# Stacked two-part operands laid out anew in a cross-attention kernel, and one context remainder moved ahead of the maxima

## The reference

```python
# layer 0: one head, width 512, masked
q = x @ Wq.T + bq;  k = y @ Wk.T + bk;  v = y @ Wv.T + bv
scores = where(mask == 0, -1e9, q @ k.T)
x1 = softmax(scores) @ v + x
# layer 1: 16 heads of 32, on x1
Q, K, V = x1 @ Wq.T + bq, y @ Wk.T + bk, y @ Wv.T + bv      # split into heads
ctx = softmax(Q @ K.T / sqrt(32)) @ V                       # heads joined again
z = ctx @ W_o.T + b_o + x1
out = (z - mean(z)) / sqrt(var(z) + 1e-5) * gamma + beta
```

## Time and profile before

| | before |
|---|---|
| time, median of 3 runs | 422.56 us (421.71 to 424.55) |
| profiled execution: its time | 420.85 us |
| profiled execution: its span | 418.9 us |
| mean granted TensorE clock | 0.989 of full |
| TensorE matmuls busy (share of span) | 391.7 us (93%) |
| VectorE, ScalarE, GpSimd busy | 288.4, 264.0, 228.2 us |

### The profile page before, as it was taken

The page is one execution under the profiler, slowest core; times in us unless marked ns, Lnnn a source line. Parts: engine busy times, 40 slices in busy tenths (PEclk is TensorE's granted clock), DMA queues, the critical chain, the costliest instruction groups (busy, mean ns, idle before and its releaser), DMA issues.

```text
span 418.9 us, 12165 instructions
## 1 busy us (share of the span) xinstructions
PE 391.7 (93%) x4968; PEld 296.9 (71%) x4968; DVE 288.4 (69%) x703; ACT 264.0 (63%) x783; POOL 228.2 (54%) x249
## 2 busy tenths in 40 slices
PE   4999998799999999999999999999999999999990
PEld 4996765577777877777777777777778776677570
DVE  0145487468866996689867986698579866557656
ACT  0443777675678665867487657856786658565620
POOL 0400368225537753785568656774377547822766
PEclk9999999999999999999999999999999999899997
DMA  8993104400042301430042205130333012330112
GB/s 256 399 359 101 50 6 129 146 4 3 2 138 87 127 2 44 181 105 26 10 172 95 76 2 170 57 126 2 126 98 127 2 30 79 101 129 2 42 58 100
DMA packets 19229, 39.44 MB, mean 94 GB/s; under 512 B 1865, under 2 KB 5449, under 8 KB 18151
## 3 DMA queue, kind: packets, MB, share of 16 engines
q1 hardware_dynamic: 18599, 37.72, 26.1%
q10 hardware_dynamic: 576, 0.96, 0.8%
HBM read 26.49 MB, written 8.39 MB: 83 GB/s over the span
## 4 chain that ended last, share of the span: by engine, by line
PE 82%; DMA 6%; ACT 5%; POOL 2%; SPq 2%; DVE 2%; issue 1%; POOLq 0%
PE ps_q L910 21%; PE ps_out L975 20%; PE ps_t L935 13%; PE ps_s L924 7%; PE ps_pv L950 7%; PE ps_out L871 4%; DMA p_b<-p_l 4%; PE ps_s L847 4%; SPq L267 2%; ACT prob L494 1%; PE ps_pv L884 1%; DMA raw<-in_w0k 1%; ACT pt L503 1%; PE ps_pv L847 1%; PE ps_s L992 1%
## 5 line engine op out<-in xcount | busy, mean ns | idle before, releaser
L344 POOL TENSOR_TENSOR prob<-prob,rc 128x308 f32<-128x308 f32 x128 | 90.6, 714 | 145.7 <-DVE rc L686 145.4
L494 ACT ACTIVATE prob<-ps_s,mx 128x77 f32<-128x77 f32 x512 | 121.2, 322 | 0.7 <-DVE mx L677 0.7
L503 ACT ACTIVATE pt<-ps_t 77x512 f32<-77x512 f32 x128 | 76.1, 594 | 66.0 <-PE ps_t L935 65.1
L684 DVE TENSOR_REDUCE sm<-prob 128x4 f32<-128x308 f32 x128 | 59.5, 465 | 38.8 <-ACT prob L494 38.7
L935 PE MATMUL ps_t<-ident,prob 128*77 128x128 f32 x512 | 79.7, 278 | 2.3 <-ACT pt L503 2.3
L935 PEld LDWEIGHTS ps_t<-ident,prob 128*77 128x77 f32 x512 | 62.2, 148 | 20.6 <-issue 6.3
L677 DVE TENSOR_REDUCE mx<-ps_s 128x4 f32<-128x308 f32 x128 | 54.7, 470 | 25.7 <-PE ps_s L924 25.7
L323 POOL TENSOR_TENSOR x_l<-x_raw,x_h 128x512 fp32r<-128x512 f32 x32 | 44.2, 1386 | 25.2 <-ACT x_h L447 15.0
L910 PE MATMUL ps_q<-x_h,wq_h 128*128 128x512 f32 x128 | 54.2, 423 | 0.0
L910 PE MATMUL ps_q<-x_h,wq_l 128*128 128x512 f32 x128 | 53.6, 419 | 0.0
L924 PEld LDWEIGHTS ps_s<-k1T,q 32*64 32x64 f32 x2048 | 25.8, 130 | 28.4 <-issue 15.3
(11 more groups left out here) (116 smaller groups left out, 599.0 us busy)
## 6 DMA issues: line engine op xcount, KB each, us to landing
x_raw<-in_xT SPq DMA_DIRECT2D x8, 1024.0 KB, 6.3
y<-in_x SPq DMA_DIRECT2D x28, 256.0 KB, 2.8
out<-y SPq DMA_DIRECT2D x28, 256.0 KB, 2.0
p_b<-p_a SPq DMA_DIRECT2D x8, 154.0 KB
mask_sb<-in_mask SPq DMA_DIRECT2D x7, 154.0 KB, 5.4
raw<-in_w0k SPq DMA_DIRECT2D x2, 512.0 KB, 6.5
raw<-in_w0q SPq DMA_DIRECT2D x2, 512.0 KB, 9.9
raw<-in_w0v SPq DMA_DIRECT2D x1, 1024.0 KB, 12.3
```

The costliest lines, as they stand in the source:

```text
L344: nc.gpsimd.tensor_tensor(ap, ap, wide(rc[:, k % 2, h], KEYS), ALU.mult).then_inc(prob_done, 1)
L494: e = nc.scalar.activation(prob[:, k % 2, h, t], ps_s[:, h, t * KEYS:(t + 1) * KEYS], ACT.Exp, bias=mx[:, k % 2, h, t:t + 1])
L503: nc.scalar.activation(pt[:, h], ps_t[0:KEYS, :], ACT.Copy).then_inc(pt_ready, 1)
L684: nc.vector.reduce_sum(sm[:, k % 2, h], prob[:, k % 2, h], AX_X).then_inc(sum_done, 1)
```

## The change

The stacks get another order of rows. The 51 rows of `_a` above the rounded part and the 26 upper rows of `_b` now hold, for p0, a second copy of the rounded part (against the remainder of U or v0), and rows 0 to 76 of `_b` hold the remainder of p0 against the rounded part of U or v0. So `p0_rest` writes the remainder straight into `p0_b` (the tile `p0_l` goes), and two moves are left, both of the rounded part. For the weights, the remainder is moved in two pieces, and the rounded part gets into rows 0 to 76 of `_b` by a second copy on VectorE (`u_b` after `u_rest`, `v0_b` after `v0_a`). In the fourth steps `ct_rest` stands ahead of the four `largest`, and `OUT_AT[3]` puts two output matmuls ahead of `transpose0` and seven into part 1, where it were four and five.

```diff
--- before.py
+++ after.py
@@ -36,7 +36,7 @@
 
 
 TURN = 2 * CH
-OUT_AT = {1: (0, 14, 18, 22), 2: (22, 28, 36, 42), 3: (42, 46, 51, 56)}
+OUT_AT = {1: (0, 14, 18, 22), 2: (22, 28, 36, 42), 3: (42, 44, 51, 56)}
 STEPS = UNITS + 2
 LAST = BLOCKS - 1
 
@@ -110,7 +110,6 @@
         stat0 = sb("stat0", [P, 3, TILES])
         p0_a = sb("p0_a", [P, 2, BLOCK], F32R)
         p0_b = sb("p0_b", [BROWS, 2, BLOCK], F32R)
-        p0_l = sb("p0_l", [KEYS, BLOCK], F32R)
         q = sb("q", [P, 2, BLOCK])
         mx = sb("mx", [P, 2, GROUP_HEADS, TILES])
         sm = sb("sm", [P, 2, GROUP_HEADS, TILES])
@@ -143,6 +142,7 @@
         ld_xT, ld_mask, ld_bo = sem("ld_xT"), sem("ld_mask"), sem("ld_bo")
         ld_x = [sem(f"ld_x{t}") for t in range(TILES)]
         ld_last = sem("ld_last")
+        u_copied, v0_copied = sem("u_copied"), sem("v0_copied")
         u_stacked, v0_stacked, p0_stacked = [sem("u_stacked0"), sem("u_stacked1")], sem("v0_stacked"), sem("p0_stacked")
         stored = [sem(f"stored{t}") for t in range(TILES)]
 
@@ -266,30 +266,26 @@
 
                 sp.dma_start(f32(to), f32(frm)).then_inc(done, 16)
 
-            def stack_weights(a, b, own, done, rounded, remaining, count):
-
-                sp.wait_ge(rounded, count)
-                move(a[KEYS:P, own], a[0:TAIL, own], done)
-                move(b[0:REST, own], a[TAIL:KEYS, own], done)
+            def stack_weights(a, b, own, done, remaining, count):
+
                 sp.wait_ge(remaining, count)
-                move(b[REST:BROWS, own], rest[:, own], done)
+                move(a[KEYS:P, own], rest[0:TAIL, own], done)
+                move(b[KEYS:BROWS, own], rest[TAIL:KEYS, own], done)
 
             def stack_probs(i, b):
 
                 if not block_exists(i, b):
                     return
                 wait(sp, p0h_ready, blocks(i, b) + 1)
-                move(p0_b[REST:BROWS, b % 2], p0_a[0:KEYS, b % 2], p0_stacked)
-                wait(sp, p0l_ready, blocks(i, b) + 1)
-                move(p0_a[KEYS:P, b % 2], p0_l[0:TAIL], p0_stacked)
-                move(p0_b[0:REST, b % 2], p0_l[TAIL:KEYS], p0_stacked)
+                move(p0_a[KEYS:P, b % 2], p0_a[0:TAIL, b % 2], p0_stacked)
+                move(p0_b[KEYS:BROWS, b % 2], p0_a[TAIL:KEYS, b % 2], p0_stacked)
 
             next_inputs(0, 0)
             stack_probs(0, 0)
-            stack_weights(u_a, u_b, slice(0, 1), u_stacked[0], u_h_ready, u_ready, 1)
-            stack_weights(v0_a, v0_b, slice(0, BATCH), v0_stacked, v0_h_ready, v0_ready, BATCH)
-
-            stack_weights(u_a, u_b, slice(1, 2), u_stacked[1], u_h_ready, u_ready, 2)
+            stack_weights(u_a, u_b, slice(0, 1), u_stacked[0], u_ready, 1)
+            stack_weights(v0_a, v0_b, slice(0, BATCH), v0_stacked, v0_ready, BATCH)
+
+            stack_weights(u_a, u_b, slice(1, 2), u_stacked[1], u_ready, 2)
             sp.wait_ge(mm_u, BATCH)
             sp.wait_ge(wq_ready, CH)
             for t in range(TILES):
@@ -628,7 +624,7 @@
                 if not block_exists(i, b):
                     return
                 wait(dve, p0h_ready, blocks(i, b) + 1)
-                nc.vector.tensor_tensor(p0_l[:], ps_pv[0:KEYS, :], f32(p0_a[0:KEYS, b % 2]),
+                nc.vector.tensor_tensor(p0_b[0:KEYS, b % 2], ps_pv[0:KEYS, :], f32(p0_a[0:KEYS, b % 2]),
                                         ALU.subtract).then_inc(p0l_ready, 1)
 
             dve.wait_ge(ld_cols, 16)
@@ -652,8 +648,9 @@
             def u_rest(b):
                 dve.wait_ge(u_h_ready, b + 1)
                 if b == 1:
-                    dve.wait_ge(v0_stacked, 48)
+                    dve.wait_ge(v0_stacked, 32)
                 nc.vector.tensor_tensor(rest[:, b], bank[5 + 2 * b][0:KEYS, :], f32(u_a[0:KEYS, b]), ALU.subtract).then_inc(u_ready, 1)
+                nc.vector.tensor_copy(u_b[0:KEYS, b], f32(u_a[0:KEYS, b])).then_inc(u_copied, 1)
 
             p0_rest(0, 0)
             u_rest(0)
@@ -664,9 +661,10 @@
             for v in range(BATCH):
                 dve.wait_ge(v0o_ready, v + 1)
                 nc.vector.tensor_copy(v0_a[0:KEYS, v], v0o[:, v]).then_inc(v0_h_ready, 1)
+                nc.vector.tensor_copy(v0_b[0:KEYS, v], v0o[:, v]).then_inc(v0_copied, 1)
             for v in range(BATCH):
                 dve.wait_ge(v0_h_ready, v + 1)
-                dve.wait_ge(u_stacked[0], 48)
+                dve.wait_ge(u_stacked[0], 32)
                 nc.vector.tensor_tensor(rest[:, v], v0o[:, v], f32(v0_a[0:KEYS, v]), ALU.subtract).then_inc(v0_ready, 1)
 
             def largest(i, k, h):
@@ -744,9 +742,12 @@
                 g, b = k % CH, k // CH
                 if g == 3:
                     residual(i, b - 1, 2)
+                if g == 3:
+                    ct_rest(i, k - 2)
                 largest(i, k, 0)
                 largest(i, k, 1)
-                ct_rest(i, k - 2)
+                if g != 3:
+                    ct_rest(i, k - 2)
                 largest(i, k, 2)
                 largest(i, k, 3)
                 if g == 3:
@@ -905,7 +906,8 @@
                         w, v = wq_h[:, c, own], x_l[:, b % 2, c]
                     else:
                         if g == 0 and m == 3 * CH:
-                            wait(pe, p0_stacked, 48 * (blocks(i, b) + 1))
+                            wait(pe, p0_stacked, 32 * (blocks(i, b) + 1))
+                            wait(pe, p0l_ready, blocks(i, b) + 1)
                         w, v = ((u_a[:, b % 2, own], p0_a[:, b % 2]), (u_b[:, b % 2, own], p0_b[:, b % 2]))[m - 3 * CH]
                     mm = nc.tensor.matmul(ps_q[:], w, v, start=(m == 0), stop=(m == QUERY - 1))
                 if last == QUERY:
@@ -1046,7 +1048,8 @@
             pe.wait_ge(u_ready, 1)
             pe.wait_ge(p0l_ready, 1)
             project(bank[5:7], raw1, ctxT_sb, mm_v1T, [ld_w1v, ld_w1v], 0, 2)
-            pe.wait_ge(u_stacked[0], 48)
+            pe.wait_ge(u_stacked[0], 32)
+            pe.wait_ge(u_copied, 1)
             query(0, 0, 3 * CH, QUERY)
             project(bank[5:7], raw1, ctxT_sb, mm_v1T, [ld_w1v, ld_w1v], 2, CH)
             pe.wait_ge(k1T_ready, CH)
@@ -1061,9 +1064,11 @@
                         output(i, b - 1, OUT_AT[g][n], OUT_AT[g][n + 1])
 
                 if type(i) is int and k == CH - 1:
-                    pe.wait_ge(u_stacked[1], 48)
+                    pe.wait_ge(u_stacked[1], 32)
+                    pe.wait_ge(u_copied, 2)
                 if type(i) is int and k == CH + 1:
-                    pe.wait_ge(v0_stacked, 48)
+                    pe.wait_ge(v0_stacked, 32)
+                    pe.wait_ge(v0_copied, BATCH)
                     pe.wait_ge(wo_ready, CH)
                 scores(i, k)
                 if type(i) is int and k == 0:
```

## The result

| | before | after |
|---|---|---|
| median of 15 runs | 423.24 us (420.59 to 425.03) | 420.07 us (418.48 to 421.75) |
| ratio after / before | | 0.9939, 95% interval 0.9919 to 0.9958 |
| profiled execution: its time, its span | 420.85, 418.9 us | 418.48, 416.5 us |

The change makes the kernel 0.6% faster, some 2.6 us (1.8 to 3.4) by the ratio; the two medians lie 3.2 apart. The profiled spans differ by 2.4.

What follows compares the result with a forecast made beforehand. TensorE carries 82% of the chain, so gains come where it stands, limited by ScalarE. -1.44 - 0.56 - 1.1 + 0.46 + 0.3 + 0.2 = -2.1 us, from 422.56 to 420.4 us (chance 0.58), range 417.4 to 423.4.

Steps and rivals of the forecast that it cites:

- `ct_rest` and `transpose0`: Fourth steps, shown on k = 11: `ct_rest` runs 159.88 to 160.56, so the 0.28 us stall before `transpose0` goes.
- The maxima's shift: Fourth steps: maxima start 0.4 us later at no cost, covered by `leave_pt`; rival that they become late, 423.5 us, chance 0.10.
- ScalarE as what is late next: ScalarE's 4.75 us from `leave_pt` of head 2 through `round_q` limits k = 11 to 0.36 gained, not TensorE's 0.6.
- Step 3: k = 3, without an output part: p0 data land sooner for the stacked matmul, gaining 1.1 us; bounds 0 and 2.4.
- Step 31: k = 31, without `transpose0` or query: two more output matmuls ahead of head 2's transposes cost 0.46 us; bounds 0.3 and 0.5.
- The second copy in step 1: End of k = 1: the VectorE copy of `u_b` for batch 1 has no cover and costs 0.3 us; low end 0.
- The stack of U: Preparation: both moves of U wait for the remainder; a loss of 0.2 us, some 0.6 by the Trainium skill.
- The rule of the Trainium skill on the number of engines: A copy uses the most engines, up to 16, dividing its rows: 3 for 51, so U's loss is some 0.6 us.
- the fourth steps: Steps 11, 15, 19 and 23 gain 0.36 us each, 1.44 together; k = 7 and k = 27 gain 0.28 each, 0.56.

Runs made afterwards that it cites:

- Order only: The kernel before with only the fourth steps' order changed (`ct_rest` ahead of the maxima, two output matmuls ahead of `transpose0`): 421.75 us, 0.9969.
- layout only: The kernel before with only the new layout (two moves, remainder in place, second copies on VectorE): 422.73 us, 1.0002.
- q first: The changed kernel with `round_q` ahead of the second `normalise` in the fourth steps: 418.03 us, 0.9893 to the kernel before.
- parts back: The changed kernel with `OUT_AT[3]` as before (four and five output matmuls): 420.02 us, 0.9939 to the kernel before.
- copying later: The changed kernel with the second copy of U for batch 1 moved from the end of step 1 into step 2: step 2 stayed at 8.48 us.
- before again: The kernel before, unchanged, profiled once more: step 16 took 10.56 us (9.22 in its first profile), step 20 9.22 us.

## Why the prediction was right, and where its sizes were off

The forecast was -2.1 us and 420.4; measured were -2.6 (1.8 to 3.4) and 420.07. By its steps:

- **`ct_rest` and `transpose0`: right.** Predicted from 159.88 to 160.56 on the clock of the kernel before, `ct_rest` ran, with the 1.56 added, from 159.88. The maxima's shift cost nothing, as `leave_pt` covered it.
- **ScalarE as what is late next: right, and shown.** Predicted 0.36 each for the steps 11 to 23 and 0.28 for 7 and 27; measured 0.37 to 0.42 and 0.30. Order only, layout only and q first agree with this and with nothing else tried.
- **Step 3: right in kind, mis-sized.** The term was 1.1, the step won 1.96. The 1.1 took the last issue as the clock of the landing and 4.20 us as a constant. The moves were issued 1.21 sooner after the scores and took 0.74 less on top. What counts is the 51-row move, which went from second place behind 77 rows to the first. With the load behind, the last update of the semaphore came 4.85 us after its issue in the kernel before and 4.13 in the changed one; in k = 27, without the load, 4.12 and 4.05. So the place alone makes hardly a difference, and what the first place saved is, in the main, the load's delay. The upper bound of 2.4 held the term.
- **Step 31: right.** Predicted 0.46, measured 0.49; undone by parts back. For the rows see below.
- **The second copy in step 1: wrong.** The 0.3 was put on the copy. It did take 0.98 us (above the cast's 0.92 of the earlier trace rows), but copying later won nothing. The 0.17 that step 2 lost came from the new wait instruction ahead of the scores, which the prediction costed at nothing.
- **The new waits in TensorE's stream: not foreseen.** They moved other work to the place in the stream where TensorE waits for instructions and cost about 1.1 us in steps 20 and 21 ("before again"). No term and no rival of the prediction had this.
- **The stack of U: no loss.** Predicted a loss of 0.2. The idle before the stacked matmul went from 0.62 to 0.57 (compare):

```profile
35.85 0.69 DVE L652 TENSOR_TENSOR rest<-ps_t,u_a 77x512 fp32r<-77x512 f32 x1 [1.96 <-ACT u_a L478]
...
36.57 0.70 SPq L267 DMA_DIRECT2D u_a<-rest  x1
...
40.66 0.50 PE L912 MATMUL ps_q<-p_a,u_a 128*128 128x512 f32 x1 [0.57 <-DMA u_b<-rest]
```

The stacked matmul itself is 0.46 later (40.66 against 40.20), but so are, by 0.52, the query matmuls that precede the stack (34.63 against 34.11). TensorE waited 0.5 longer for the first weights in this execution (6.4 us against 5.9), which is not of the change. The rule of the Trainium skill on the number of engines would have made it a loss of 0.6, and at this place that was not seen: the 51-row move went from first of three to first of two, and the 77-row move that went away behind it may have made up for the later issue, which was not tried. Elsewhere the rule was the better guide: a sum built on it would have tied the landing of step 3 to the 51-row move.

For k = 31, the rows after that answer to the earlier trace rows, the transposes of head 1 and 2 and `leave_pt` of head 2 (2.85 us are to be added to compare):

```profile
382.78 0.63 PE L937 MATMUL ps_t<-ident,prob 128*77 128x128 f32 x4 [0.30 <-ACT pt L499]
...
384.88 0.60 PE L937 MATMUL ps_t<-ident,prob 128*77 128x128 f32 x4
...
385.51 0.59 ACT L499 ACTIVATE pt<-ps_t 77x512 f32<-77x512 f32 x1 [0.62 <-PE ps_t L937]
```

The transposes of head 1 wait for `leave_pt`, those of head 2 start at 384.88, 4.42 after the scores (380.46), where it was 3.94 before.

The sum of these steps is -3.5, more than the -2.4 of the spans. The first scores came 0.44 later in this execution. Steps 16 and 20 were 2.7 longer, of which the part in step 20 is of the change, and 21 and 29 were 2.1 shorter, of which 1.6 is the stretch at the lower clock in the profile of before. So the nearness of -2.1 to the measured -2.6 is in good part luck: step 3 was too small by 0.86, the fourth steps by 0.2, the copies and U too dear by 0.4, and against these 1.4 us stands the loss of about 1.1 in steps 20 and 21 that was not foreseen. With that loss the steps give -2.4, which agrees with the timed runs (-1.8 to -3.4).

## What to carry to other kernels

Before a stall is counted as a gain, follow the other engine's chain through the same step: here the copy of q ended 0.14 us before the scores that a DMA held up, so it became the limit as soon as the DMA was out of the way, and one line of order (q ahead of a `normalise` that nobody waits for) was worth another 0.24 us per step. When several DMAs share a semaphore, find the one that lands last, not the one issued last; another row count (45 and 32 here in place of 51 and 26) and the slow piece first are cheap to have. Count what a change adds to the longest instruction stream, and compare every step of the two profiles, not only those that the change was made for: the loss in step 20 is as large as half of what step 3 won. A step that lacks part of the pattern (31 here) should be checked by itself when the pattern is rearranged.

## What the runs showed of the hardware that was not expected

- A 51-row move of 102 KB inside the core landed 3.8 to 5.1 us after its issue, one of 45 rows (90 KB) after 2.6; a 1 MB load issued behind it made 1.3 us of difference for the former. The 51 rows had 3 updates of the semaphore of their own, 26 rows 13.
- A fulfilled wait instruction on TensorE's queue, between the wait that ended last and the first matmul, cost 0.15 us.
- The cast of 77 x 512 numbers took 0.41 us alone and 0.98 beside a multiplication of GpSimd. The Trainium skill, "SBUF — State Buffer", section "SBUF: two separate sides", says that the two engines share a port pair which one holds for a whole instruction; the two numbers agree with that.
- TensorE stood at a fixed instruction of its stream until 1.2 to 1.6 us after a packet of 16 KB of instructions had landed: for 0.8 to 1.7 us in step 16 in twelve of thirteen profiles. The next stop stands 1280 instructions further on, and there six added waits put it on work that is wanted sooner.
